# A fused attention and mixture-of-experts layer: expert blocks in four passes instead of two, with 48 instead of 32 tiles of sums beside them, and a shorter plan

## The chip, the cores and the metric

The kernel runs on one core of one Trainium2 chip. The metric is device time in microseconds (us), the median of the runs shown; lower is better. The engines are TensorE (PE, its weight loads PEld), VectorE (DVE), ScalarE (ACT), GpSimd (POOL) and SyncE (SP), which here only issues DMAs.

## The reference

The input x is 16 batches of 512 tokens of 256 values, float32. With `xn = layernorm(x)` the output is

```python
out = x + attention(xn) + moe(xn)
# attention: 16 heads of 16, rope, causal softmax, output projection
# moe, for all 8192 tokens:
scores = softmax(flat @ router_w.T + router_bias)            # 32 experts
topk_scores, topk_idx = top_k(scores, 4); topk_scores /= topk_scores.sum()
h = silu(x @ gate_w[e].T) * (x @ up_w[e].T)                  # hidden width 128
out = sum over the 4 chosen e of topk_score * (h @ down_w[e].T)
out += (silu(flat @ sgate_w.T) * (flat @ sup_w.T)) @ sdown_w.T   # shared expert, width 512
```

## The kernel before

`P` is 128, `E` 32 experts, `TOPK` 4, `TOKENS` 8192, `SEQ` 512, `NT` 4 tiles of 128 tokens in a batch.

**Phase A** (`phase_a`) runs the 16 batches one after the other, in an order of steps written out by hand (`ORDER`, and `LAST_ORDER` for the last batch). Each batch gets layernorm, attention, the shared expert and the router. x plus attention plus the shared expert goes to `sum_dram` in device memory. The router's steps `route`, `rank`, `rankA`, `rankB` and `rankC` find for each token and choice a row of `values`, where every expert has a region of its own; four indirect DMAs of GpSimd per tile (line 537) write the normalized token, its destination row and its weight there. A row's place within a region is the number of tokens that chose this expert before: TensorE counts them (`rank`), and VectorE keeps the totals in `both`: `counts` (all tokens so far, line 850) and `early` (those of the first 4096 tokens, line 848, with the mask `in_half` of line 825). `base = counts + region` is line 824.

**The plan** is the head of `phase_bc` (lines 1314 to 1351 and 1422 to 1469). From the two rows of counts it works out, on one row of 288 columns, where each of the `NBLOCK` = 288 blocks of 128 rows starts in `values` (`place`) and which expert it belongs to (`expert`). There are `VE = 2 * E` = 64 runs, one for each half of the tokens and each expert. `past[v, n]` says whether block n lies past the start of run v; three matmuls with one output row (lines 1347 to 1349) sum it over the runs, with one semaphore after the last. Then 14 small VectorE instructions, each waiting for the one before, turn the sums into `place` and `expert` (lines 1450 to 1469) and raise `ready`. SyncE and TensorE start when `ready` is up.

**Stage C**, the blocks, follows in the same function. Block n: SyncE loads its 128 rows (line 1218, four places at a time, up to 16 blocks ahead: it waits until block n - 16 has been scattered); TensorE transposes them (1358), multiplies by the expert's gate and up weights (1369), ScalarE takes tanh (1274), VectorE gates and weights (1483 to 1489), TensorE transposes (1377) and multiplies by the down weights (1383), ScalarE copies the result (1288) and GpSimd scatters it by rows to `y_dram` (1329), four rows for each token. All experts' weights lie in SBUF, so a change of expert loads nothing. The loop has 16 blocks ahead, 8 iterations of `BODY` = 32 blocks (`LOOPS` = 8), and 16 blocks behind.

The first half's runs are done after at most `HBLOCK` = 160 blocks. So from iteration `H0` = 5 on, beside every fourth block, one of the first `HTILE` = 32 **tiles of sums** is taken (`tile_half`, `out_half`, lines 1227 to 1242; `half_a`, `half_b`, `half_c`, 1493 to 1506): SyncE loads the tile's four expert results (512 KB) and its row of `sum_dram` (128 KB), VectorE adds them in three instructions, SyncE stores 128 KB to `out`. 8 tiles fall in each of the iterations 5, 6 and 7, and 8 beside the last 16 blocks.

```python
H0 = HBLOCK // BODY
PER = BODY // 4
assert (LOOPS - H0) * PER + PER == HTILE
```

In the same loops `sums_part` loads the sums of the other half of the tokens into SBUF (`sums_in`, four tiles in each iteration).

**Stage D** (`phase_d`) follows all of it. For the other 32 tiles SyncE loads `ys` (line 1561, 512 KB each, four buffers), VectorE adds in three instructions (1582, 1584, 1588) and ScalarE's queue stores `res` to `out` (1569).

Of the kernel before, what the change touches and what calls it, by code (L numbers as in the profile page):

```python
# [34 lines left out]
P = 128  # L35
# [24 lines left out]
HTOK = TOKENS // 2  # L60
HTILE = HTOK // P
HBLOCK = HTOK * TOPK // P + E
# [118 lines left out]
def block_kernel(nc, x, wqkvr, wo, wgu_s, wd_s, bias, wgu_e, wd_e, rope_cos, rope_sin, out):  # L181
# [5 lines left out]
    with ctx:  # L187
# [9 lines left out]
        both = sb("both_counts", [P, 2, E])  # L197
        early, counts = both[:, 0, :], both[:, 1, :]
# [7 lines left out]
        phase_a(nc, sb, sem, ident, iota_e, both, we_gu, we_d, ps_g, ps_u, ps_av, x, wqkvr, wgu_e, wd_e, wo, wgu_s, wd_s, bias,  # L206
                rope_cos, rope_sin, values, sum_dram)
        phase_bcd(nc, sb, sem, ident, iota_e, both, we_gu, we_d, ps_g, ps_u, ps_av, values, sum_dram, y_dram, out)


def phase_a(nc, sb_, sem, ident, iota_e, both, we_gu, we_d, ps_g, ps_u, ps_av, x, wqkvr, wgu_e, wd_e, wo, wgu_s, wd_s, bias,
            rope_cos, rope_sin, values, sum_dram):
    stack = ExitStack()
    early, counts = both[:, 0, :], both[:, 1, :]
    with stack:
# [100 lines left out]
        in_half = sb("in_half", [P, 1])  # L316
# [145 lines left out]
        def _(pool):  # L462
# [25 lines left out]
            const(pool.memset(both[:], 0.0))  # L488
# [180 lines left out]
        def _(dve):  # L669
            front = Chain(dve, dve_front, 2 + 3 + 3 * 3 + 6 + 8, passed_dve)  # L670
# [126 lines left out]

            def route(b, step, env):
# [41 lines left out]
            def rank_b(b, step, env):  # L840
# [279 lines left out]
def phase_bcd(nc, sb_, sem, ident, iota_e, both, we_gu, we_d, ps_g, ps_u, ps_av, values, sum_dram, y_dram, out):  # L1120
    outer = ExitStack()
    with outer:

        sums = sb_("sums_in", [P, HTILE, D], F32, outer)
        stored_h = [sem(f"stored_h{i}") for i in range(NSUM)]
        phase_bc(nc, sb_, sem, ident, iota_e, both, we_gu, we_d, ps_g, ps_u, ps_av, values, sum_dram, y_dram, sums, out, stored_h)
        phase_d(nc, sb_, sem, y_dram, sums, out, stored_h)
# [5 lines left out]
def phase_bc(nc, sb_, sem, ident, iota_e, both, we_gu, we_d, ps_g, ps_u, ps_av, values, sum_dram, y_dram, sums, out, stored_h):  # L1133
    stack = ExitStack()
    with stack:
# [5 lines left out]
        VE = 2 * E  # L1141
        nb_i = sb("nb_i", [P, 2, E], I32)
        nb_f = sb("nb_f", [P, 2, E])
        run_r = sb("run_r", [P, 3, VE])
        first_r = sb("first_r", [P, VE + 1])
        nb_c = sb("nb_c", [VE, 4])
        tri = sb("tri", [VE, VE])
# [38 lines left out]
        H0 = HBLOCK // BODY  # L1186
        PER = BODY // 4
        assert NBLOCK == 2 * NR + LOOPS * BODY and HBLOCK == H0 * BODY
        assert (LOOPS - H0) * PER + PER == HTILE

# [13 lines left out]
        def _(sp):  # L1204
# [15 lines left out]
            def sums_part(i):  # L1220

                nt = HTILE // LOOPS
# [21 lines left out]
            def loop_part(i, tiles, second):  # L1244
                for k in range(BODY):
                    stage(i * BODY + NR + k, k % NR, False)
                    if k == NR:
                        sums_part(i)
                    if tiles and k % 4 == 0:
                        tile_half((i - H0) * PER + k // 4, k // 4, second and k < 4 * NYS, second)  # L1250
# [7 lines left out]
            for n in range(NBLOCK - NR, NBLOCK):  # L1258
                stage(n, n % NR, False)
                if n % 2 == 0:  # L1260
                    s = (n - (NBLOCK - NR)) // 2
                    tile_half(HTILE - PER + s, s, False, False)
# [51 lines left out]
        def _(pool):  # L1314
# [317 lines left out]
```

## Time and profile before

| what | before |
|---|---|
| median of 3 runs | 1873.74 us (1872.81 to 1875.88) |
| the profiled execution's own time | 1873.05 us |
| its span, first to last instruction | 1871.2 us |
| phase A, until the last sums are stored | 0 to about 1273 us |
| the plan, first row of counts to `ready` | 1276.4 to 1290.2 us |
| first to last block (first tanh to last scatter) | 1297.7 to 1796.2 us |
| stage D, first load issued to the end | 1805.4 to 1871.2 us |
| mean granted TensorE clock | 0.955 of full speed |

The profile is one execution of the program, recorded by the hardware. Busy time is given for each engine, the idle time before an instruction with what ended it. TensorE's two levels of clock are 1.2 and 2.4 GHz; a granted clock of 0.5 is the lower one. A matmul's end is modelled, so a busy TensorE is not one at its peak.

### The profile page before, as it was taken

The page shows a single profiled execution, that of the slowest core. Times are in us where ns is not written, and L with a number is a line of the kernel's source. Part 1 is how long each engine was busy: PE and PEld are TensorE (multiplying, and loading weights), DVE is VectorE, ACT ScalarE, POOL GpSimd, SP SyncE. Part 2 cuts the span into 40 slices and gives each one's busy share as a digit, 9 for nine tenths or more (in the row PEclk, how much of TensorE's full clock was granted, in tenths as well). Part 3 has the DMA queues.
Part 4 walks back from the last instruction along what each step waited for, and adds up shares of the span by engine and source line. Part 5 has one row for each costly group of instructions (what it writes and reads, how often), then busy time and mean ns, then how long its engine had stood idle before and what let it go on. Part 6 is the DMA issues. An engine that isn't in the chain of part 4 may idle for free. (4 is left out here: it accounts for less than half of the span.)

```text
span 1871.2 us, 43234 instructions
## 1 busy us (share of the span) xinstructions
PE 1697.6 (91%) x11827; PEld 1052.2 (56%) x11828; DVE 1358.2 (73%) x3501; ACT 794.2 (42%) x1667; POOL 710.4 (38%) x716
## 2 busy tenths in 40 slices
PE   4999999999999999999999999686999999999930
PEld 2455554554555545545555455344877888777720
DVE  5977878779778797797887977534666666777857
ACT  2544445344453454444534544231444444444410
POOL 5433423334233243342332433301555565555520
PEclk8999999999999999999999999767999999999975
DMA  7273561743725617437266173684555555788958
GB/s 144 76 127 58 112 113 42 128 70 90 124 54 114 93 58 135 62 98 124 46 119 83 70 130 60 153 229 148 165 166 154 165 174 171 244 259 255 299 185 315
DMA packets 171641, 253.18 MB, mean 135 GB/s; under 512 B 25269, under 2 KB 121406, under 8 KB 171584
## 3 DMA queue, kind: packets, MB, share of 16 engines
q1 hardware_dynamic: 128256, 168.34, 42.5%
q0 software_dynamic: 26112, 67.42, 9.8%
q10 hardware_dynamic: 17216, 16.78, 3.0%
q8 instruction: 21, 0.34, 0.1%
q14 instruction: 36, 0.29, 0.1%
HBM read 112.54 MB, written 92.70 MB: 110 GB/s over the span
## 5 line engine op out<-in xcount | busy, mean ns | idle before, releaser
L752 DVE TENSOR_REDUCE neg<-ps_u 128x2 f32<-128x768 f32 (+3 forms) x384 | 389.7, 1042 | 65.2 <-PE ps_u L1009 60.4
L537 POOL DMA_INDIRECT values<-we_gu,slot x256 | 250.0, 977 | 381.9 <-ACT we_gu L609 227.9
L1329 POOL DMA_INDIRECT y_dram<-yb_all,xg x288 | 283.5, 984 | 235.2 <-issue 162.9
L987 PE MATMUL ps_g<-we_gu 128*128 128x512 f32 x512 | 251.9, 620 | 0.0
L629 ACT ACTIVATE probs<-ps_u 128x1024 f32<-128x1024 f32 x160 | 160.3, 1023 | 166.9 <-PE ps_u L1050 166.9
L1003 PE MATMUL ps_u<-k_st,q_st 48*128 48x128 f32 (+3 forms) x1024 | 177.5, 392 | 39.3 <-ACT we_d L629 26.9
L629 ACT ACTIVATE we_d<-ps_u 128x1024 f32<-128x1024 f32 x160 | 159.4, 1021 | 111.1 <-PE ps_u L1050 100.6
L527 POOL TENSOR_TENSOR we_gu<-we_d,we_gu 128x512 fp32r<-128x512 f32 x64 | 81.9, 1290 | 286.1 <-ACT we_gu L577 286.1
L1003 PEld LDWEIGHTS ps_u<-k_st,q_st 48*128 48x128 f32 x1024 | 88.0, 189 | 156.0 <-DVE neg L752 74.6
L1383 PE MATMUL ps_u<-we_d,h_t 128*128 x576 | 175.2, 386 | 0.0
L1036 PE MATMUL ps_u<-q_st,k_st 50*128 50x512 f32 (+3 forms) x1024 | 158.9, 375 | 8.5 <-DVE neg L752 2.9
L1036 PEld LDWEIGHTS ps_u<-q_st,k_st 50*128 50x128 f32 x1024 | 83.8, 190 | 143.2 <-issue 52.2
L1369 PE MATMUL ps_g<-we_gu,x_t 128*128 x576 | 150.7, 384 | 4.7 <-issue 4.7
L1369 PE MATMUL ps_av<-we_gu,x_t 128*128 x576 | 150.2, 383 | 1.6 <-issue 1.4
L1483 DVE TENSOR_SCALAR wh<-xg 128x1 f32<-128x1 f32 x288 | 44.3, 154 | 142.6 <-ACT tnh L1274 120.6
L601 ACT ACTIVATE we_gu<-ps_g 128x512 f32<-128x512 f32 x64 | 37.8, 591 | 231.6 <-PE ps_g L987 231.6
L987 PEld LDWEIGHTS ps_g<-we_gu 128*128 128x128 f32 x512 | 89.1, 191 | 80.5 <-issue 75.7
L1476 DVE COPY x_t<-ps_g 128x256 f32<-128x256 f32 x288 | 120.5, 418 | 10.1 <-PE ps_g L1358 8.2
L968 PE MATMUL ps_g<-we_gu 128*128 128x512 f32 x256 | 126.5, 617 | 0.0
L1080 PE MATMUL ps_u<-w_d,hid 128*128 128x256 f32 x512 | 125.6, 395 | 0.0
L1288 ACT ACTIVATE yb_all<-ps_u 128x256 f32<-128x256 f32 x288 | 110.6, 384 | 33.8 <-PE ps_u L1383 8.0
L518 POOL TENSOR_TENSOR we_d<-we_d 128x512 f32<-128x512 f32 x64 | 81.8, 1279 | 106.9 <-DVE we_d L722 104.0
(188 smaller groups left out, 2892.3 us busy)
## 6 DMA issues: line engine op xcount, KB each, us to landing
xg<-values SPq DMA_DIRECT2D x288, 129.0 KB
q_st<-we_gu SPq DMA_DIRECT2D x192, 128.0 KB, 4.1
k_st<-we_gu SPq DMA_DIRECT2D x192, 128.0 KB, 6.5
ys_h<-y_dram SPq DMA_DIRECT2D x32, 512.0 KB
ys<-y_dram SPq DMA_DIRECT2D x32, 512.0 KB, 5.4
we_gu<-x SPq DMA_DIRECT2D x16, 512.0 KB
xres<-x SPq DMA_DIRECT2D x16, 512.0 KB, 9.7
sum_dram<-osum SPq DMA_DIRECT2D x16, 512.0 KB, 9.2
```

The source lines that it names most:

```text
L537: pool.indirect_dma_start(values[:, :], bass.IndirectOffsetOnAxis(ap=slot[:, k:k + 1], axis=0), xs[:, t % 2, j, :], None).then_inc(scatter ...
L629: nc.scalar.activation(probs[g % 2][:, u, :], ps_u[env[1][step][0]][:, :, :].rearrange("p a n -> p (a n)"), ACT.Exp, scale=SCALE).then_inc ...
L752: nc.vector.tensor_reduce(neg[:, g % 2, i, :, k0:k0 + nk], ps[:, :, 0:nk * n].rearrange("p a (k n) -> p a k n", n=n), AX.X, ALU.max, negat ...
L968: ins = nc.tensor.matmul(ps[:, :], w_qkvr[:, c, lo:lo + P], xn_t[:, c, :], start=(c == 0), stop=(c == KC - 1))
L987: ins = nc.tensor.matmul(ps[:, :], w_gu[:, c, lo:lo + P], xn_t[:, c, :], start=(c == 0), stop=(c == KC - 1))
L1003: nc.tensor.matmul(ps[:, a, k * n:(k + 1) * n], q_st[rows, h, i * P:(i + 1) * P], k_st[rows, h, 0:n], start=(k == 0), stop=False, skip_gro ...
L1036: nc.tensor.matmul(ps[:, a, lo:lo + n], k_st[rows, h, kt * P:(kt + 1) * P], q_st[rows, h, kt * P:SEQ], start=(lo == 0), stop=False, skip_g ...
L1080: nc.tensor.matmul(ps[:, t // 2, (t % 2) * D:(t % 2 + 1) * D], hid[:, m, t * P:(t + 1) * P], w_d[:, m, :], start=(t % 2 == 0 and m == 0), ...
L1329: pool.indirect_dma_start(y_dram[:, :], bass.IndirectOffsetOnAxis(ap=ent[k][:, 0:1], axis=0), yb[k][:, :], None, bounds_check=TOKENS * TOP ...
L1369: ins = nc.tensor.matmul(ps_gu[s][:, 0:2 * HE], x_t[s][:, c * P:(c + 1) * P], w_gu[:, bass.ds(e, 1), c, :], start=(c == 0), stop=(c == KC ...
L1383: nc.tensor.matmul(ps_y[s][:, 0:D], h_t[s][:], w_d[:, bass.ds(e, 1), :], start=True, stop=True).then_inc(y_ps, 1)
L1476: nc.vector.tensor_copy(x_t[s][:], ps_x[s][:, 0:D]).then_inc(xt_sb, 1)
```

## The change

- Stage C takes the blocks in four equal passes of four batches (`MARKS` = 4, 8, 12, 16 batches) instead of two halves. A pass takes, for each expert, the blocks that its tokens have filled up to the mark. The number of blocks stays 288. 
- The tiles of sums start in iteration `H0` = 3 instead of 5, still one beside every fourth block: `HTILE` is 48 instead of 32, 8 in each of the iterations 3 to 7 and 8 beside the last 16 blocks. Stage D has `LTILE` = 16 tiles instead of 32, and `sums_part` loads two tiles in each iteration instead of four.
- Phase A keeps the counts after each batch in `seen[:, b + 1, :]`, addressed by the loop's register, instead of `early` and `counts`. Lines 825 and 848 go, with one link of VectorE's chain.
- The plan has `VE` = 128 runs. Its arithmetic per run (the step from one run to the next, in blocks and in experts) stands in columns of 128 values (`step_e`, `step_p` by GpSimd; `col_p`, `col_m` by VectorE), and four matmuls, each with a semaphore count of its own, give the sums of these. 7 VectorE instructions on the row of 288 follow instead of 14.

```diff
-HTOK = TOKENS // 2
+MARKS = (4, 8, 12, BATCH)
+NPASS = len(MARKS)
+HTOK = MARKS[-2] * SEQ
 HTILE = HTOK // P
-HBLOCK = HTOK * TOPK // P + E
+LTILE = TOKENS // P - HTILE
...
-        both = sb("both_counts", [P, 2, E])
-        early, counts = both[:, 0, :], both[:, 1, :]
+        seen = sb("seen", [P, BATCH + 1, E])
...
+            def seen_by(b):
+                return seen[:, bass.ds(b, 1), :].rearrange("p o e -> p (o e)")
...
-                front.link(b, nc.vector.tensor_tensor(base[:], counts[:], region[:], ALU.add))
-                front.link(b, nc.vector.tensor_scalar(in_half[:], dest_f[:, 0:1], float(HTOK * TOPK), None, ALU.is_lt))
+                front.link(b, nc.vector.tensor_tensor(base[:], seen_by(b), region[:], ALU.add))
...
-                new = ps_g[bank][:, NT * E:(NT + 1) * E]
-                nc.vector.scalar_tensor_tensor(out=early[:], in0=new, scalar=in_half[:, 0:1], in1=early[:], op0=ALU.mult,
-                                               op1=ALU.add)
-                nc.vector.tensor_tensor(counts[:], counts[:], new, ALU.add
+                nc.vector.tensor_tensor(seen_by(b + 1), seen_by(b), ps_g[bank][:, NT * E:(NT + 1) * E], ALU.add
                                         ).then_inc(S["ranked"], 1)
...
-        VE = 2 * E
+        VE = NPASS * E
...
-        H0 = HBLOCK // BODY
-        PER = BODY // 4
-        assert (LOOPS - H0) * PER + PER == HTILE
+        H0, EVERY = 3, 4
+        PER, LAST = BODY // EVERY, NR // 2
+        assert (LOOPS - H0) * PER + LAST == HTILE
+
+        def block_of(t):
+            return NR + H0 * BODY + EVERY * t if t < HTILE - LAST else NBLOCK - NR + 2 * (t - (HTILE - LAST))
+        for lo, hi in zip((0,) + MARKS, MARKS[:-1]):
+            assert block_of(lo * NT) // 4 * 4 >= hi * NT * TOPK + E + NR
...
-                nt = HTILE // LOOPS
+                nt = LTILE // LOOPS
...
+            pool.memset(step_e[:], 1.0).then_inc(c_pool, 1)
             pool.memset(tri[:], 0.0).then_inc(c_pool, 1)
-            pool.wait_ge(c_pool, 5)
+            pool.wait_ge(c_pool, 6)
 
             pool.affine_select(out=tri[:], in_=tri[:], compare_op=ALU.is_ge, fill=1.0, base=-1,
                                pattern=[[-1, VE]], channel_multiplier=1).then_inc(c_pool, 1)
+            for p in range(1, NPASS):
+                pool.affine_select(out=step_e[:], in_=step_e[:], compare_op=ALU.not_equal, fill=float(1 - E),
+                                   base=1 - E * p, pattern=[[0, 1]], channel_multiplier=1).then_inc(c_pool, 1)
+                pool.wait_ge(c_pool, 7 + p)
+            pool.affine_select(out=step_p[:], in_=step_e[:], compare_op=ALU.not_equal, fill=float(4 * BLANK // RB),
+                               base=1 - VE, pattern=[[0, 1]], channel_multiplier=1).then_inc(c_pool, 1)
+            pool.affine_select(out=step_e[:], in_=step_e[:], compare_op=ALU.not_equal, fill=0.0,
+                               base=1 - VE, pattern=[[0, 1]], channel_multiplier=1).then_inc(c_pool, 1)
...
-            pe.wait_ge(plan, 4)
-            nc.tensor.matmul(ps_g[0][0:1, 0:NBLOCK], one_c[:], past[:], start=True, stop=True)
-            nc.tensor.matmul(ps_av[0:1, 0:NBLOCK], nb_c[:, 2:3], past[:], start=True, stop=True)
+            pe.wait_ge(plan, 5)
             nc.tensor.matmul(ps_g[2][0:1, 0:NBLOCK], nb_c[:, 1:2], past[:], start=True, stop=True).then_inc(plan_pe, 1)
+            nc.tensor.matmul(ps_av[0:1, 0:NBLOCK], col_m[:], past[:], start=True, stop=True).then_inc(plan_pe, 1)
+            nc.tensor.matmul(ps_g[0][0:1, 0:NBLOCK], col_p[:], past[:], start=True, stop=True).then_inc(plan_pe, 1)
+            nc.tensor.matmul(ps_g[1][0:1, 0:NBLOCK], step_e[:], past[:], start=True, stop=True).then_inc(plan_pe, 1)
...
+            dve.wait_ge(c_pool, 7 + NPASS + 1)
+            dve.wait_ge(plan, 2)
+            nc.vector.scalar_tensor_tensor(out=col_p[:], in0=step_p[:], scalar=float(RB), in1=nb_c[:, 1:2], op0=ALU.mult,
+                                           op1=ALU.subtract)
+            nc.vector.tensor_scalar(col_m[:], step_e[:], float(-RB), None, ALU.mult).then_inc(plan, 1)
+            dve.wait_ge(plan, 3)
+            nc.vector.scalar_tensor_tensor(out=col_m[:], in0=nb_c[:, 2:3], scalar=3.0, in1=col_m[:], op0=ALU.mult,
+                                           op1=ALU.add)
...
+            link(nc.vector.scalar_tensor_tensor(out=row_f[:, 0, :], in0=blk_i[0:1, :], scalar=float(-CB),
+                                                in1=ps_g[2][0:1, 0:NBLOCK], op0=ALU.add, op1=ALU.is_ge))
+            dve.wait_ge(plan_pe, 4)
+            link(nc.vector.scalar_tensor_tensor(out=row_f[:, 1, :], in0=ps_av[0:1, 0:NBLOCK], scalar=float(E * RB - CB),
+                                                in1=row_f[:, 0, :], op0=ALU.add, op1=ALU.mult))
+            link(nc.vector.tensor_tensor(row_f[:, 1, :], row_f[:, 1, :], blk_i[0:1, :], ALU.add))
+            dve.wait_ge(plan_pe, 5)
+            link(nc.vector.tensor_tensor(row_f[:, 1, :], row_f[:, 1, :], ps_g[0][0:1, 0:NBLOCK], ALU.add))
             link(nc.vector.tensor_scalar(row_f[:, 1, :], row_f[:, 1, :], float(BLANK), None, ALU.min))
+            nc.vector.tensor_copy(place[:], row_f[:, 1, :])
+            dve.wait_ge(plan_pe, 6)
+            nc.vector.tensor_copy(expert[:], ps_g[1][0:1, 0:NBLOCK]).then_inc(ready, 1)
...
-        NTILE = HTILE
+        NTILE = LTILE
```

## Rows read from the trace of the kernel before

**Rows 1.** The page: busy time by engine; granted clock in 40 slices, in tenths
```profile
PE 1697.6 (91%) x11827; PEld 1052.2 (56%) x11828; DVE 1358.2 (73%) x3501; ACT 794.2 (42%) x1667; POOL 710.4 (38%) x716
...
PEclk8999999999999999999999999767999999999975
```

**Rows 2.** The chain of waits from 1780 us on: shares of the chain by line
```profile
by line: DMA ys<-y_dram 36.2%; DVE red L1582 12.7%; DVE red L1584 8.1%; DVE res L1588 5.0%; issue 4.4%; DVEq L1588 0.9%; SPq L1561 0.5%; DVEq L1583 0.4%; DVEq L1552 0.3%; DVEq L1581 0.3%
```

**Rows 3.** Windows: length, busy (count) of PE, PEld, DVE, ACT, POOL; PEclk, DMA share, GB/s
```profile
1433.57:1488.20 54.63, 53.32 (x290) 44.10 (x290) 33.27 (x128) 26.77 (x97) 31.48 (x33) 1.00 0.53 164
...
1597.28:1652.73 55.45, 54.14 (x289) 44.00 (x289) 43.09 (x152) 26.76 (x96) 31.41 (x33) 1.00 0.81 250
1652.73:1708.08 55.35, 54.03 (x289) 44.01 (x289) 43.14 (x152) 26.89 (x96) 31.59 (x33) 1.00 0.79 252
1708.08:1764.95 56.87, 55.86 (x296) 45.09 (x296) 44.44 (x157) 27.79 (x99) 31.79 (x33) 1.00 0.92 290
...
1793.75:1809.20 15.45, 0.00 (x0) 0.00 (x0) 0.00 (x0) 0.01 (x1) 1.97 (x2) 0.62 0.20 70
1809.22:1837.90 28.68, 0.00 (x0) 0.00 (x0) 23.97 (x48) 0.00 (x0) 0.00 (x0) 0.50 0.97 348
```

**Rows 4.** Timeline, VectorE, stage D: start us, length us, instruction [idle before <-releaser]
```profile
1809.22 0.69 DVE L1582 TENSOR_TENSOR red<-ys 128x512 f32<-128x512 f32 x1 [16.62 <-DMA ys<-y_dram]
...
1834.27 0.68 DVE L1582 TENSOR_TENSOR red<-ys 128x512 f32<-128x512 f32 x1
...
1835.90 0.68 DVE L1582 TENSOR_TENSOR red<-ys 128x512 f32<-128x512 f32 x1
...
1837.93 0.69 DVE L1582 TENSOR_TENSOR red<-ys 128x512 f32<-128x512 f32 x1 [0.32 <-DMA ys<-y_dram]
...
1866.95 0.68 DVE L1582 TENSOR_TENSOR red<-ys 128x512 f32<-128x512 f32 x1
```

**Rows 5.** Timeline of all engines through the plan
```profile
1276.36 0.80 DVE L1429 TENSOR_SCALAR nb_f<-both_counts 128x64 f32<-128x64 f32 x1 [3.48 <-PEq L215]
...
1277.26 0.23 POOL L1323 TENSOR_SCALAR_AFFINE_SELECT tri<-tri 64x64 f32<-64x64 f32 x1
...
1281.01 1.12 PE L1347 MATMUL ps_g<-yb_all,one_c 64*1 64x288 f32 x2 [0.64 <-DVE yb_all L1447]
...
1282.88 1.16 PE L1349 MATMUL ps_g<-yb_all,nb_c 64*1 64x288 f32 x2
...
1284.08 0.44 DVE L1450 TENSOR_TENSOR yb_all<-yb_all,ps_g 1x288 f32<-1x288 f32 x1 [3.13 <-PE ps_g L1349]
...
1288.87 0.30 DVE L1466 TENSOR_SCALAR yb_all<-yb_all 1x288 f32<-1x288 f32 x1
...
1289.87 0.30 DVE L1469 CAST expert<-yb_all 1x288 int32<-1x288 f32 x1
```

**Rows 6.** Timeline of VectorE in one batch of phase A, where counts are taken
```profile
1074.09 0.19 DVE L824 TENSOR_TENSOR base<-both_counts,region 128x32 f32<-128x32 f32 x1
1074.31 0.15 DVE L825 TENSOR_SCALAR in_half<-dest_f 128x1 f32<-128x1 f32 x1
...
1081.92 0.29 DVE L830 TENSOR_REDUCE zs<-exo 128x4 f32<-128x128 f32 x1 [3.19 <-ACT exo L634]
...
1084.76 0.28 DVE L845 TENSOR_TENSOR pos<-ps_g,base 128x128 f32<-128x128 f32 x1
1085.08 0.25 DVE L848 SCALAR_TENSOR_TENSOR both_counts<-ps_g,in_half,both_counts 128x32 f32<-128x32 f32 x1
...
1088.22 0.72 DVE L773 STREAM_TRANSPOSE av<-ps_av 128x512 f32<-128x512 f32 x1 [2.80 <-PE ps_av L1068]
```

**Rows 7.** Line 1588, VectorE's sequencer: count, duration in ns (min/median/max)
```profile
L1588 DVEq FUSED_REGOPS  x28: 57/57/57, 1817.1 to 1868.1; - x28
```

**Rows 8.** Line 1329, GpSimd: 1400 to 1560 us, without tiles
```profile
L1329 POOL DMA_INDIRECT y_dram<-yb_all,xg x94: 982/984/992, 1400.3 to 1559.1; - x94
```

**Rows 9.** The same line from 1600 to 1760 us, with tiles
```profile
L1329 POOL DMA_INDIRECT y_dram<-yb_all,xg x94: 982/984/1107, 1599.4 to 1759.8; - x94
```

More of the change, by code:

```diff
@@ L204, in block_kernel, with phase_a @@
         ps_av = ctx.enter_context(nc.psum_tensor("ps_av", [P, 512], F32))
-        phase_a(nc, sb, sem, ident, iota_e, both, we_gu, we_d, ps_g, ps_u, ps_av, x, wqkvr, wgu_e, wd_e, wo, wgu_s, wd_s, bias,
+        phase_a(nc, sb, sem, ident, iota_e, seen, we_gu, we_d, ps_g, ps_u, ps_av, x, wqkvr, wgu_e, wd_e, wo, wgu_s, wd_s, bias,
                 rope_cos, rope_sin, values, sum_dram)
-        phase_bcd(nc, sb, sem, ident, iota_e, both, we_gu, we_d, ps_g, ps_u, ps_av, values, sum_dram, y_dram, out)
-def phase_a(nc, sb_, sem, ident, iota_e, both, we_gu, we_d, ps_g, ps_u, ps_av, x, wqkvr, wgu_e, wd_e, wo, wgu_s, wd_s, bias,
+        phase_bcd(nc, sb, sem, ident, iota_e, seen, we_gu, we_d, ps_g, ps_u, ps_av, values, sum_dram, y_dram, out)
+def phase_a(nc, sb_, sem, ident, iota_e, seen, we_gu, we_d, ps_g, ps_u, ps_av, x, wqkvr, wgu_e, wd_e, wo, wgu_s, wd_s, bias,
             rope_cos, rope_sin, values, sum_dram):
     stack = ExitStack()
-    early, counts = both[:, 0, :], both[:, 1, :]
+    counts = seen[:, BATCH, :]
     with stack:
@@ L315, in phase_a @@
         dest_f = sb("dest_f", [P, NT * TOPK])
-        in_half = sb("in_half", [P, 1])
         xs = in_gu([P, 2, TOPK, ROW])
@@ L487, in _ @@
                             allow_small_or_imprecise_dtypes=True))
-            const(pool.memset(both[:], 0.0))
+            const(pool.memset(seen[:], 0.0))
             const(pool.memset(over[:], 0.0))
@@ L1146, in phase_bc @@
         nb_c = sb("nb_c", [VE, 4])
+        step_e = sb("step_e", [VE, 1])
+        step_p = sb("step_p", [VE, 1])
+        col_p = sb("col_p", [VE, 1])
+        col_m = sb("col_m", [VE, 1])
         tri = sb("tri", [VE, VE])
@@ L1185, in phase_bc @@
         LOOPS = (NBLOCK - 2 * NR) // BODY
-        H0 = HBLOCK // BODY
-        PER = BODY // 4
-        assert NBLOCK == 2 * NR + LOOPS * BODY and HBLOCK == H0 * BODY
-        assert (LOOPS - H0) * PER + PER == HTILE
+        H0, EVERY = 3, 4
+        PER, LAST = BODY // EVERY, NR // 2
+        assert NBLOCK == 2 * NR + LOOPS * BODY
+        assert (LOOPS - H0) * PER + LAST == HTILE
[3 more added lines that the diff above has]
+            assert block_of(lo * NT) // 4 * 4 >= hi * NT * TOPK + E + NR
         def expert_loop(eng, stage):
@@ L1248, in loop_part @@
                         sums_part(i)
-                    if tiles and k % 4 == 0:
-                        tile_half((i - H0) * PER + k // 4, k // 4, second and k < 4 * NYS, second)
+                    if tiles and k % EVERY == 0:
+                        q = k // EVERY
+                        tile_half((i - H0) * PER + q, q % NSUM, second and q < NYS, second and q < NSUM)
             for n in range(NR):
@@ L1428, in link @@
                 dve.wait_ge(dchain, n_[0])
-            link(nc.vector.tensor_scalar(nb_f[:], both[:], float(P - 1), None, ALU.add))
+            link(nc.vector.tensor_scalar(nb_f[:], seen[:, MARKS[0]:BATCH + 1:MARKS[0], :], float(P - 1), None, ALU.add))
             link(nc.vector.tensor_copy(nb_i[:], nb_f[:]))
@@ L1466, in _ @@
             link(nc.vector.tensor_scalar(row_f[:, 1, :], row_f[:, 1, :], float(BLANK), None, ALU.min))
-            link(nc.vector.tensor_copy(place[:], row_f[:, 1, :]))
-            link(nc.vector.tensor_scalar(row_f[:, 0, :], row_f[:, 3, :], float(E - 1), None, ALU.min))
-            nc.vector.tensor_copy(expert[:], row_f[:, 0, :]).then_inc(ready, 1)
+            nc.vector.tensor_copy(place[:], row_f[:, 1, :])
+            dve.wait_ge(plan_pe, 6)
+            nc.vector.tensor_copy(expert[:], ps_g[1][0:1, 0:NBLOCK]).then_inc(ready, 1)
@@ L1511, in loop_part @@
                     stage(i * BODY + NR + k, k % NR, False)
-                    if tiles and k % 4 < 3:
-                        [half_a, half_b, half_c][k % 4]((i - H0) * PER + k // 4, k // 4)
+                    if tiles:
+                        q = k // EVERY
+                        t, s = (i - H0) * PER + q, q % NSUM
+                        if k % EVERY == 0:
+                            half_a(t, s)
+                        elif k % EVERY == 1:
+                            half_b(t, s)
+                        if k % EVERY == min(2, EVERY - 1):
+                            half_c(t, s)
             front(0, 0, True)
```

50 lines of the change are left out of this document (18 added, 32 removed).

## The prediction

> **What bounds the kernel now.** I read the page first. TensorE is busy 91% of the span, VectorE 73%, and the granted clock is full except in three slices around 1220 to 1320 us and at the very end [rows 1]. An average over the span says little here: the change touches the counts of phase A, the plan, the blocks and stage D, and each has a limit of its own.
>
> The chain that ended last lies wholly in stage D: 36.2% of what it covers is the wait for the loads of `ys`, the rest VectorE's three additions for each tile [rows 2]. TensorE, ScalarE and GpSimd do nothing in that stage; only the DMA engines (0.97 busy, 348 GB/s) and VectorE work [rows 3]. So a tile of stage D costs its full time, and a tile beside the blocks costs only what it adds to them.
>
> The windows of stage C are cut at the tanh of blocks 16, 48, 80 and so on, one window for each iteration of 32 blocks. Iteration 2 (from 1433.57 us) has no tiles and takes 54.63 us; TensorE is busy 53.32 us of it, with VectorE at 33.27 us and the DMA engines at 0.53. The four other iterations without tiles are as long within 0.25 us. Iterations 5, 6 and 7 carry 8 tiles each: 55.45, 55.35 and 56.87 us, VectorE at 43 to 44 us, DMA at 0.79 to 0.92 [rows 3]. TensorE bounds the blocks with and without tiles.
>
> Between the phases the plan is one serial chain, during which TensorE waits: its first row instruction starts at 1284.08 us, when the third matmul is done, and the last starts at 1289.87 us [rows 5].
>
> **The change, part by part.** The sum is made against the profiled execution's own time, 1873.05 us, 1.85 us above its span; the median shown is 0.69 us above it.
>
> *Stage D: 16 tiles fewer.* The first addition starts at 1809.22 us, the 16th tile's at 1835.90, the 32nd's at 1866.95 [rows 4]. What stands before the first (a gap of 15.45 us from the last result copied to the first addition, nearly empty [rows 3]) and after the last stays. If stage D is cut after its 16th tile, 1866.95 - 1835.90 = 31.05 us go. Bounds: the fastest a tile can be is where the data is there, from 1834.27 to 1835.90, 1.63 us, VectorE's own pace; 15 such steps are 24.5 us, and of the 57.73 us now 33.2 would go. The slowest 15 steps are those of the second half, 1837.93 to 1866.95, 29.02 us: 28.7 us would go. I take 31.05, because the new stage starts from idle queues just as the old one's first half does.
>
> *Stage C: 16 tiles more.* Iterations 3 and 4 become what 5 and 6 are now: the same 8 tiles, 24 additions and 8 times 768 KB. That is 55.40 - 54.63 = 0.77 us each, 1.5 us in all. The upper end is iteration 7, 56.87 - 54.63 = 2.24 us each, 4.5 in all; but its second half holds also the loads for the last 16 blocks, which take a tile for every second block, and SyncE runs up to 16 blocks ahead. The lower end is 0: `sums_part` moves half as much. SyncE's queue gains in each iteration 8 stores, which wait for VectorE's addition, and the rows for later blocks are queued behind them; in iterations 5 and 6 the same waits cost no more than the 0.77 us, since the blocks' rows are loaded up to 16 ahead. The order of the blocks changes, with four runs of each expert instead of two; no weights are loaded for a run, so I cost it at nothing.
>
> *The plan.* Before, the first of the three matmuls started at 1281.01 us and they followed each other at half of 1282.88 - 1281.01, 0.94 us; the first took 1.12 us [rows 5]. Let t be the start of the first. Before, `ready` rose at 1289.87 + 0.30, t + 9.16. Now each matmul signals for itself, ready at t + 1.1, 2.1, 3.0 and 4.0. The first row instruction starts at t + 1.15; a linked one costs 0.48 us, as from 1284.08 over the ten steps to 1288.87 [rows 5]. The second starts with the second matmul at t + 2.1, the third follows at 2.6, the fourth at 3.1 (the third matmul is done), the minimum at 3.55, the copy of `place` at 3.9, and the copy of `expert`, after the fourth matmul, at about 4.1, done by 4.6. So t + 4.6 instead of t + 9.2: 4.6 us less. Against it: eight instructions ahead of t work on 64 columns more. A column costs (0.28 - 0.19) / 96, 0.9 ns, by lines 845 and 824 [rows 6], so 8 times 64 columns are 0.5 us. The two or three small instructions for `col_p` and `col_m` (0.15 us each, as line 825) stand where VectorE waits for the matmul with `tri`; some 0.1 us may stick out. GpSimd's five added selects run beside VectorE: at 0.23 us as line 1323 and some 0.15 us for each wait they end near 1279.2 us, 0.7 us before VectorE needs them. That makes -4.0 us. Bounds: -5.0 (the wider rows cost nothing), and -2.5, if GpSimd is 1.5 us slower than that.
>
> *Phase A.* Lines 825 and 848 go. Their room on VectorE is 0.20 us (1074.31 to the next at 1074.51) and 0.16 us (1085.08 to 1085.24) in each batch. But VectorE idles right behind both places, 3.19 us for ScalarE's exponentials before line 830 and 2.80 us for TensorE before line 773 [rows 6], so nothing comes of it. If all of it did, 16 times 0.36 = 5.8 us would go. Three operands now take their address from a register; the nearest row is the register arithmetic of line 1588, 57 ns [rows 7], so at most 16 times 3 times 0.057 = 2.7 us would come, hidden by the same idle time. I take 0.
>
> *Sum:* -31.05 + 1.5 - 4.0 + 0 = -33.5 us, 1873.05 - 33.5 = 1839.5 us. With half of the 0.69 us to the median I give 1840.
>
> *One rule against the change.* GpSimd's scatter instruction takes 984 ns at the median without tiles [rows 8] and 984 ns with them, at most 1107 [rows 9], although VectorE is busy about 9.8 us more in an iteration there (43.09 against 33.27 [rows 3]), all of it additions with two SBUF inputs. The Trainium skill says otherwise for such a pair (SBUF — State Buffer, "Who interferes with whom"): a VectorE instruction with two SBUF inputs contends with a GpSimd instruction that reads SBUF, and the second to start is blocked until the first is done. By that rule each of the new additions could stand behind a scatter. It is the last rival below, priced from rows.
>
> **Rivals.**
>
> *A. The extra tiles cost more.* All five iterations with tiles become like iteration 7, because the DMA engines (0.92 there) are the ones that stretch a block. Then 3 and 4 cost 4.5 us, and 5 and 6 another 1.5 each: 6.0 us above my term, 1845.5 us. For it speaks that iteration 7 exists; against it that 5 and 6, with the same tiles, stay at 0.8 [rows 3].
>
> *B. TensorE's clock moves.* Over the last batch of phase A and the plan the granted clock is 0.6 to 0.7 on average, that is partly at 1.2 and partly at 2.4 GHz [rows 1]. A slightly different timing of VectorE may shift these stretches by some us of TensorE work either way: 1833 or 1847 us, by 7 us, about a sixth of one slice of 46.8 us. The runs shown are 3 us apart already.
>
> *C. Slower.* The lock on a shared port decides. VectorE's additions for tiles and GpSimd's scatters collide in iterations 3 and 4: 16 tiles, 48 additions, each held up by a scatter of 0.98 us [rows 8] and passed on to TensorE in full. That is 47 us, and 1839.5 - 1.5 + 47 gives 1885 us. It decides from 33.5 + 1.5 = 35 us on, 0.73 us for each addition. Against it: 24 additions cost an iteration 0.77 us in all today, 0.03 us each [rows 3], and the scatters are as long with them as without [rows 9].
>
> *D. No change.* Stage D would have to be bound by something that is not its tiles, such as the stores waiting for their end. Its chain shows loads and additions alone [rows 2], so this is barely possible: 1873 us.
>
> **How the numbers follow.** My forecast 0.79, A 0.09, B 0.09, C 0.02, D 0.01. The terms' bounds, taken together as if independent, give about 6 us below and 5 above 1839.5; with B's 7 us the range is 1833 to 1847, which takes in A. A measurement of this kernel tells 0.2% (3.7 us) from no change. Faster by more than that: 0.79 + 0.09 + 0.09 = 0.97; the same 0.01; slower 0.02.
>
> **What the new profile would show.** Stage D with 16 instructions of line 1582's kind, some 27 us from the first to the last; iterations 3 to 6 at about 55.4 us each; `ready` about 4 us earlier, counted from the plan's first instruction, with the row instructions starting 3 us before the last matmul's end; phase A ending within some us of 1273. I am wrong if an iteration with tiles takes over 57 us, if the plan's first row instruction is held up by GpSimd, if a tile in stage D takes 2 us or more, or if the batches of phase A change by more than 0.3 us each.

## The result and the profile after

| | before | after |
|---|---|---|
| median, with the kernel before run beside it | 1874.81 us (4 runs) | 1857.05 us (4 runs, 1853.3 to 1861.08) |
| the profiled execution's own time | 1873.05 us | 1861.08 us |
| its span | 1871.2 us | 1859.2 us |

The ratio is 0.9903, with a 95% interval of 0.988 to 0.9925. The change makes the kernel 17.8 us faster, where 33.5 were forecast; 1857 lies outside the range of 1833 to 1847. The profiled execution of the changed kernel is the longest of its four, 4.0 us above the median, so the stages below add up to 12.0 us and not to 17.8.

The page, its span, busy times and granted clock (before in [rows 1]):

```profile
span 1859.2 us, 43225 instructions
...
PE 1704.5 (92%) x11829; PEld 1054.9 (57%) x11830; DVE 1349.1 (73%) x3465; ACT 793.5 (43%) x1667; POOL 711.8 (38%) x722
...
PEclk8999999999999999999999999876899999999995
```

Windows of the changed kernel's stage C, one for each iteration (2, 3, 4, 5 and 6), columns as in [rows 3]:

```profile
1396.68:1451.09 54.41, 53.29 (x290) 44.21 (x290) 33.24 (x128) 26.79 (x97) 31.31 (x33) 1.00 0.53 160
1505.36:1560.48 55.12, 54.00 (x290) 44.10 (x289) 43.11 (x152) 26.78 (x96) 31.81 (x33) 1.00 0.83 257
1560.48:1616.18 55.70, 54.40 (x290) 44.07 (x289) 43.13 (x152) 26.99 (x96) 31.47 (x33) 1.00 0.82 254
1616.18:1671.62 55.44, 53.70 (x289) 43.88 (x288) 43.05 (x152) 26.66 (x96) 31.59 (x33) 1.00 0.85 272
1671.62:1727.24 55.62, 54.30 (x290) 44.15 (x290) 43.02 (x152) 26.93 (x96) 31.44 (x33) 1.00 0.84 259
```

Iteration 2 has no tiles. Iterations 3 and 4 now carry them, at 55.12 and 55.70 us; before, 5 and 6 took 55.45 and 55.35 [rows 3]. All eight iterations together took 438.8 us before and take 440.0 now.

Stage D, VectorE's timeline: the first and the last of the 16 tiles.

```profile
1827.78 0.69 DVE L1607 TENSOR_TENSOR red<-ys 128x512 f32<-128x512 f32 x1 [16.21 <-DMA ys<-y_dram]
...
1854.91 0.69 DVE L1607 TENSOR_TENSOR red<-ys 128x512 f32<-128x512 f32 x1
```

27.1 us from the first to the last, where [rows 4] has 57.73 for 32: 30.6 us less.

The plan, timeline of all engines:

```profile
1298.09 0.42 DVE L1448 TENSOR_SCALAR nb_f<-seen 128x128 f32<-128x128 f32 x1 [6.23 <-PEq L216]
...
1300.84 0.19 POOL L1341 TENSOR_SCALAR_AFFINE_SELECT step_e<-step_e 128x1 f32<-128x1 f32 x1
...
1302.87 0.37 DVE L1474 TENSOR_SCALAR yb_all<-yb_all,nb_c 128x288 f32<-128x288 f32 x1
...
1303.29 1.12 PE L1365 MATMUL ps_g<-yb_all,nb_c 128*1 128x288 f32 x2 [0.65 <-DVE yb_all L1474]
...
1304.45 0.44 DVE L1476 SCALAR_TENSOR_TENSOR yb_all<-yb_all,ps_g 1x288 f32<-1x288 f32 x1 [1.21 <-PE ps_g L1365]
...
1305.48 0.45 DVE L1479 SCALAR_TENSOR_TENSOR yb_all<-ps_av,yb_all 1x288 f32<-1x288 f32 x1 [0.59 <-PE ps_av L1366]
...
1307.47 0.44 DVE L1487 CAST expert<-ps_g 1x288 int32<-1x288 f32 x1
```

From the start of the first matmul with one output row (1303.29) to the end of `expert` (1307.91) it is 4.62 us; it was 9.16 [rows 5]. VectorE's first row instruction starts right after the first of the four matmuls and not after the last. GpSimd's last select starts at 1300.84, ahead of the columns' first use. From the plan's first instruction to that matmul it is 5.20 us; it was 4.65. The whole plan took 13.81 us and takes 9.82.

So far nothing is missing. It is missing in phase A. Its last instruction, before and after:

```profile
1272.18 0.69 DVE L794 TENSOR_TENSOR osum<-ps_u,xres 128x512 f32<-128x512 f32 x1 [1.03 <-PE ps_u L1089]
```

```profile
1291.17 0.69 DVE L794 TENSOR_TENSOR osum<-ps_u,xres 128x512 f32<-128x512 f32 x1 [1.03 <-PE ps_u L1088]
```

Phase A ends 19.0 us later. The first instruction of the plan then waits 6.23 us for the end of the phase instead of 3.48 [rows 5]; the trace names no more than TensorE's sequencer for it. The changed kernel's last step from `base` to `base`, that is from one batch to the next (line 827 there, 824 before):

```profile
1090.01 0.19 DVE L827 TENSOR_TENSOR base<-seen,region 128x32 f32<-128x32 f32 x1
...
1104.14 0.72 DVE L773 STREAM_TRANSPOSE av<-ps_av 128x512 f32<-128x512 f32 x1 [2.84 <-PE ps_av L1067]
...
1125.28 1.41 DVE L683 BATCH_NORM_STATS2 stats<-we_gu 128x6 f32<-128x256 f32 x4 [0.70 <-DMA we_gu<-x]
...
1166.73 0.18 DVE L827 TENSOR_TENSOR base<-seen,region 128x32 f32<-128x32 f32 x1
```

And the same part of an earlier batch of the kernel before, the next `base` of which is at 1074.09 [rows 6]:

```profile
998.94 0.18 DVE L824 TENSOR_TENSOR base<-both_counts,region 128x32 f32<-128x32 f32 x1
...
1033.40 1.40 DVE L683 BATCH_NORM_STATS2 stats<-we_gu 128x6 f32<-128x256 f32 x4
```

The two steps are 76.72 and 75.15 us long, but they are not the same one: the last step before took 76.53. Over all 15 steps the median goes from 75.17 to 76.33 us and the sum from 1120.1 to 1135.5. So 15.3 of the 19.0 us come in the loop; 0.8 come ahead of its first `base` and 2.9 in the last batch, behind its last. The counts' own instructions are shorter, as expected, and the idle time behind them longer: line 773 waits 2.84 us where it waited 2.80 [rows 6]. The loss is elsewhere: line 683, the first instruction of the layernorm of the next batch, now waits for the load of x. All waits for DMAs between 100 and 1160 us, before and then after (engine, line, what it waited for: us in total, times, longest):

```profile
ACT we_gu L609 <- DMA values<-we_gu,slot: 32.7, 16, 3.4
...
DVE stats L683 <- DMA we_gu<-x: 0.2, 1, 0.2
```

```profile
ACT we_gu L609 <- DMA values<-we_gu,slot: 48.5, 15, 4.2
...
DVE stats L683 <- DMA we_gu<-x: 12.2, 14, 2.0
```

And the copies between SBUF tensors that fill `q_st` and `k_st` (line 415), which stand ahead of the sums, `xres` and x on SyncE's queue. Time from issue to landing, before and then after:

```profile
DMA to landing us min/median/max: 2.9/5.3/7.7
```

```profile
DMA to landing us min/median/max: 3.2/5.6/8.1
```

Nothing in the change touches these copies, except where they lie. `seen` takes 2176 bytes of each partition where `both` took 256, so every tensor of phase A allocated later begins 1920 bytes further on in SBUF.

### The profile page after: what moved, and what is told of

It is laid out like the page before. It is cut to its first block and busy times, and to the rows that moved or that the text cites. A ratio compares the mean times of both kernels' runs of the same rounds, so it can differ in the third digit from the quotient of the medians.

```text
span 1859.2 us, 43225 instructions
## 1 busy us (share of the span) xinstructions
PE 1704.5 (92%) x11829; PEld 1054.9 (57%) x11830; DVE 1349.1 (73%) x3465; ACT 793.5 (43%) x1667; POOL 711.8 (38%) x722
## 3 DMA queue, kind: packets, MB, share of 16 engines
q1 hardware_dynamic: 130816, 170.44, 44.4%
```

## The experiments

Three theories. **L** (layout): the addresses make the copies slower, and what is queued behind them comes late. **V**: the counts' new instructions, addressed from a register and in another place of VectorE's order, cost the time. **C**: the profile of the changed kernel is from a slower moment or chip.

The runs fall in groups with a time of the kernel before beside each. In two groups it took 1875 to 1876 us, as in the first measurement; in three it took 1970 to 1980 us. The runs carry the number of their chip: 0 and 3 for the first two, 14, 8 and 8 for the other three. So the level goes with the chip as far as it was seen, but no chip was seen at both levels and only one was used twice; that the chip causes it is not shown. I compare within a group alone.

### Where the kernel before takes 1970 to 1980 us

**The kernel before, unedited** (e0_control).

> The kernel before, unedited, for a profile of it from the same chip as the runs beside it. Theory L (the 1920 bytes that the counts grew by move every later SBUF tensor, and the SBUF-to-SBUF copies into q_st and k_st run slower from the new addresses): batches of phase A last 75.15 us as in the first profile, and the load of x is waited for almost nowhere. Theory C (the profile of the changed kernel comes from a slower chip or moment): batches last about 76.3 us here too, and VectorE's line 683 waits for the load of x. Time by L 1873 to 1878 us with the copies at 5.3 us median to landing; by C the same time on a slower chip, with 5.6 us.

Measured: 1981.05 us beside 1980.26. Its batches last 82.3 us at the median. The longest waits that no other engine or DMA in the profile ends, and the one for the scatters:

```profile
ACT neg_t L620 <- remote: 75.4, 11, 8.0
...
DVE neg L752 <- remote: 49.6, 15, 4.4
...
ACT we_gu L609 <- DMA values<-we_gu,slot: 4.6, 3, 3.4
```

In one batch VectorE stands still for 4.28 us ahead of line 752, and ScalarE for 3.10 us beside it:

```profile
998.50 0.19 DVE L824 TENSOR_TENSOR base<-both_counts,region 128x32 f32<-128x32 f32 x1
...
1039.40 0.96 DVE L752 TENSOR_REDUCE neg<-ps_u 128x2 f32<-128x768 f32 x1 [4.28 <-remote]
```

The view names the releaser "remote", which says no more than that. I read it so that these stalls cover much of what comes late behind the copies: line 683 waits for x only once, in the first batch. No run tests this reading.

**The kernel before with shifted tensors** (e1_before_shift1920 and, in the next group, f1_before_shift1920).

```diff
         both = sb("both_counts", [P, 2, E])
+        shift = sb("shift", [P, 480])
```

> The kernel before with 1920 unused bytes behind the counts, so that every later SBUF tensor of phase A lies where the changed kernel has it, and nothing else. Theory L: the batches grow from 75.15 to about 76.3 us and the whole by 14 to 18 us, ratio to before 1.008 to 1.010. Theory C and theory V (the cost comes from the counts' new instructions, their addresses from a register or their new place in VectorE's order): no change, ratio 0.998 to 1.002.

> The kernel before with 1920 unused bytes behind the counts, again. Where the kernel before takes some 1874 us, theory L expects batches of 76.3 us and 1888 to 1892 us, ratio 1.007 to 1.010, with the copies' 2048-byte packets at a mean of 260 ns instead of 253; theory V (the counts' instructions) 1874 us, ratio 1.000. Where it takes some 1980 us both expect 1.000, as measured.

Measured: 1.0006 (0.9983 to 1.0029) and 1.0002 (0.9979 to 1.0026). No cost here. By time alone theory L would have fallen; it stood because of the packets' duration, below.

**The changed kernel with 128 bytes more** (e2_after_shift128, f2_after_shift128), which puts each later tensor of phase A 2048 bytes beyond its old place:

```diff
         seen = sb("seen", [P, BATCH + 1, E])
+        shift = sb("shift", [P, 32])
```

> The changed kernel with 128 unused bytes behind the counts, so that the later tensors of phase A lie exactly 2048 bytes beyond their place in the kernel before, at the same offset from each multiple of 512. Theory L, if alignment is what matters: batches of 75.1 us again, the whole at about 1840 us, ratio 0.981 to 0.984. Theory V or C: as the changed kernel, ratio about 0.990.

> The changed kernel with 128 unused bytes behind the counts, again. Where the kernel before takes some 1874 us, theory L expects batches of 75.1 us, 1838 to 1842 us, ratio 0.981 to 0.983, packets at 253 ns; theory V 1857 us, 0.990. Where it takes some 1980 us both expect 0.984.

**The changed kernel itself** (f0_after).

> The changed kernel itself beside the others of this group. Where the kernel before takes some 1874 us: about 1857, ratio 0.990, batches of 76.3 us. Where it takes some 1980 us, as in the first group: theory L expects the misplaced SBUF tensors to cost nothing there, because other waits cover them, so -31 for stage D, -4 for the plan and +1.5 for stage C: ratio 0.983 to 0.985.

Measured: 0.9841 (0.9793 to 0.989) and 0.9852 (0.9823 to 0.9881) with the 128 bytes, 0.9856 (0.9829 to 0.9884) without. At this level the changed kernel gains 27 us as it is and 28 to 30 us with the 128 bytes; the intervals overlap, so the 128 bytes give nothing that can be told. The late x isn't covered altogether: in f0 line 683 still waits for it 6 times between 100 and 1160 us, 4.6 us in all, against 12.2 us in 14 batches at the other level.

**Two passes** (e3_two_passes, and h3_two_passes_shift128 with the 128 bytes as well): the counts and the plan of the change, without its tiles.

```diff
-MARKS = (4, 8, 12, BATCH)
+MARKS = (8, BATCH)
...
-        H0, EVERY = 3, 4
+        H0, EVERY = 5, 4
```

> The changed kernel with two passes instead of four (marks at batches 8 and 16, tiles of sums from iteration 5 on, 32 of them): what is left of the change are the counts of phase A in one tensor of 17 rows and the shorter plan. The addresses of phase A are those of the changed kernel. Theory L and theory V both expect batches of 76.3 us, so +17 us, and the plan -4 us: ratio 1.006 to 1.008. Theory C: -4 us, ratio 0.997 to 0.999.

> Two passes instead of four, with the 128 unused bytes: phase A's new counts and the shorter plan, at addresses like those of the kernel before. Theory L and the working of the prediction: only the plan's 4 us go, batches of 75.15 us, ratio 0.997 to 0.999 where the kernel before takes some 1874 us. If the counts' instructions cost or save more than 2 us over the batches, the ratio leaves that.

Measured: 0.9962 (0.9938 to 0.9986) and 0.9967 (0.9948 to 0.9986), 7 to 8 us less than before. The plan's 4 us lie inside both intervals. For e3 theories L and V both had 1.006 to 1.008, and both missed; only C's 0.997 to 0.999 comes near. But at this level a shift that costs 13.6 us at the other (g1, below) can't be measured either, so neither of these two runs can speak against V.

**All copies at multiples of 512 bytes** (f4_after_all512): the 128 bytes, and

```diff
-        bias_bc = sb("bias_bc", [P, E])
...
-        row_p = sb("row_p", [P, 1])
...
-        w_qkvr = in_gu([P, KC, 3 * D + E])
...
         parts = in_gu([P, NPART, NCH, SEQ])
+        w_qkvr = in_gu([P, KC, 3 * D + E])
...
         v_pad = sb("v_pad", [P, NT, NH, 2 * DH])
+        bias_bc = sb("bias_bc", [P, E])
+        row_p = sb("row_p", [P, 1])
```

> The changed kernel with 128 unused bytes behind the counts, the bias and one small column moved behind v_pad and the weights w_qkvr behind parts, so that parts, q_st and k_st all start at a multiple of 512 bytes. If the copies' speed goes by the offset within 512 bytes, their packets fall below 253 ns and the time is that of the kernel with 128 bytes or up to 5 us less; if only some offsets are bad and the kernel before has none of them, the two are the same within 2 us.

Measured: 0.9867 (0.9843 to 0.9892), the same as the others in time; its packets are in the table below.

**One side at a time** (h1_q512: the moves of `bias_bc` and `row_p` without that of `w_qkvr`; h2_parts512: that of `w_qkvr` alone), one execution each.

> The changed kernel with 128 unused bytes behind the counts and the bias and one column moved behind v_pad, so that the copies' destinations q_st and k_st start at a multiple of 512 bytes and their source parts stays 256 bytes beyond one. Packets of 2048 bytes took 253 ns with (source, destination) at (256, 160) beyond a multiple of 512, 260 at (128, 32), 246 at (0, 0). If the destination alone sets the speed: 246 ns here. If the source alone: 253. If both add: 249 to 250.

> The same with the source alone at a multiple of 512 (w_qkvr behind parts) and the destinations 160 bytes beyond one. Source alone sets it: 246 ns. Destination alone: 253. Both add: 249 to 250.

Measured: 1935.44 and 1936.55 us, a single run of each, which the spread of several us in this group makes useless as a time. Their packets count.

### Where the kernel before takes 1875 us

**The kernel before with shifted tensors** (g1_before_shift1920), the edit of e1.

> The kernel before with 1920 unused bytes behind the counts. Where the kernel before takes some 1874 us: theory L 1888 to 1892 us, ratio 1.007 to 1.010, batches of 76.3 us, line 683 waiting for x; theory V 1.000. Where it takes some 1980 us: 1.000, as twice measured.

Measured: 1889.64 us beside 1876.09, ratio 1.0073 (1.0056 to 1.009): 13.6 us slower by 1920 unused bytes. Its waits for DMAs, and its longest step from batch to batch (76.73 us; the median of the 15 is 76.37; line numbers are one higher):

```profile
ACT we_gu L610 <- DMA values<-we_gu,slot: 45.7, 16, 3.7
...
DVE stats L684 <- DMA we_gu<-x: 9.7, 13, 0.8
```

```profile
933.80 0.18 DVE L825 TENSOR_TENSOR base<-both_counts,region 128x32 f32<-128x32 f32 x1
...
1010.53 0.18 DVE L825 TENSOR_TENSOR base<-both_counts,region 128x32 f32<-128x32 f32 x1
```

The signature is that of the changed kernel: x is waited for 13 times, the scatters 45.7 us. Theory V has nothing to say here, for this kernel has none of the counts' new instructions. C falls too, since the kernel before runs beside it at its usual time.

**The changed kernel with 128 bytes more** (g2_after_shift128), the edit of e2.

> The changed kernel with 128 unused bytes behind the counts. Where the kernel before takes some 1874 us: theory L 1838 to 1842 us, ratio 0.981 to 0.983; theory V 0.990. Where it takes some 1980 us: 0.985, as twice measured.

Measured: 1842.38 us, ratio 0.9824 (0.9808 to 0.9841). All of the change is still there, 128 bytes are added, and 15 us are back (1857.05 less 1842.38, each with its own runs of the kernel before beside it). Waits for DMAs, and one step from batch to batch (75.15 us; the median is 75.17, as in the kernel before):

```profile
ACT we_gu L610 <- DMA values<-we_gu,slot: 33.6, 16, 3.4
```

```profile
1000.37 0.19 DVE L828 TENSOR_TENSOR base<-seen,region 128x32 f32<-128x32 f32 x1
...
1075.52 0.18 DVE L828 TENSOR_TENSOR base<-seen,region 128x32 f32<-128x32 f32 x1
```

No wait for x is left between 100 and 1160 us. The two times are of different groups, but the next run, in this same group and with the changed kernel's addresses, has a ratio of 0.9895.

**x ahead of xres** (g3_after_x_first): the changed kernel with SyncE's two loads exchanged.

```diff
+                    if env[0].get((("xT", 0), 0)):
+                        x_load(b + 1)
                     sp.wait_ge(S["sums"], 2 * b)
                     sp.dma_start(xres[:, :, :], tokens(x, b)).then_inc(x_res, 16)
-                    if env[0].get((("xT", 0), 0)):
-                        x_load(b + 1)
```

> The changed kernel with SyncE's two loads of a batch exchanged: the next batch's x is queued ahead of xres, so it lands some 1 to 3 us earlier behind the slower copies. Theory L (copies slower by address, then x late, then VectorE's statistics late): where the kernel before takes some 1874 us, the batches return to about 75.2 us and the whole to 1840, ratio 0.981 to 0.983. Theory V (the counts' instructions themselves): as the changed kernel, 0.990. Where the kernel before takes some 1980 us: as the changed kernel there, 0.986, since line 683 waits for x nowhere.

Measured: 1856.44 us, ratio 0.9895 (0.9878 to 0.9912): nothing gained, so theory L as I had put it was wrong in its last link. The waits show the second path:

```profile
ACT we_gu L609 <- DMA values<-we_gu,slot: 47.7, 16, 3.7
...
DVE gth L731 <- ACT we_gu L601: 15.1, 14, 1.5
```

Line 683 no longer waits for x. But ScalarE's line 609, which fills the rows to be scattered, waits for GpSimd's scatters as long as in the changed kernel (47.7 us; 48.5 there, 32.7 in the kernel before), then line 601 comes late, and VectorE waits for it at line 731: 15.1 us in 14 batches, where it was 2.5 us in 5. The changed kernel's page gives the packets of both as shares of the same 16 DMA engines: 44.4% of their span for the queue with the copies, 10.0% for the scatters'. I read it so that two waits stand beside each other behind one backlog, and taking one out brings up the other.

**Both mends** (g5_all512_x_first), f4's moves and g3's.

> Both mends together: the changed kernel with parts, q_st and k_st at multiples of 512 bytes and x loaded ahead of xres. Where the kernel before takes some 1874 us, 1835 to 1840 us, ratio 0.979 to 0.982, by theory L; 0.989 by theory V. Where it takes some 1980 us, 0.984 to 0.987 by both.

Measured: 1841.59 us, ratio 0.9815 (0.9798 to 0.9831), the same as with the 128 bytes alone. The wait for the scatters falls further, to 28.2 us, and nothing comes of it: once the copies are as fast as before the change, faster ones give phase A nothing that can be measured.

**Which side of the copies** (i1_src128_dst160, i2_src256_dst32). i1 has the 128 bytes behind `we_d` in place of `seen`; i2 has them behind `seen`, and `bias_bc` behind `v_pad`.

> The changed kernel with 128 unused bytes behind we_d: the source parts stays where the changed kernel has it, 128 bytes beyond a multiple of 512, and the destinations q_st and k_st go back to 160 bytes beyond one, as in the kernel before. If the source's place causes the slower copies, packets stay at 260 ns, and where the kernel before takes some 1874 us the time stays near 1857, ratio 0.990. If the destination's place does, 253 ns and 1842 us, 0.982.

> The reverse: source parts back at 256 bytes beyond a multiple of 512, destinations at 32 bytes beyond one as in the changed kernel. If the source's place causes the slower copies, 253 ns and (before at 1874) 1842 us; if the destination's does, 260 ns and 1857 us.

Measured: 1845.25 us, 0.9839 (0.9821 to 0.9856), and 1852.82 us, 0.988 (0.9862 to 0.9898). Waits for DMAs of i1 and then of i2:

```profile
ACT we_gu L610 <- DMA values<-we_gu,slot: 37.4, 16, 3.5
```

```profile
ACT we_gu L610 <- DMA values<-we_gu,slot: 44.0, 16, 3.6
...
DVE stats L684 <- DMA we_gu<-x: 8.8, 14, 0.9
```

With the destination put back, the wait for x is gone; with the source put back, it stays. The edits move other tensors too: i1 puts back all that is allocated behind `we_d`, and i2 leaves off its old place what lies between `bias_bc` and `v_pad`. Of the tensors that DMAs write in every batch, `xres` is at its old offset in i2, and x, which lies in `we_gu`, is at its new one in i1; `q_st` and `k_st` alone go with the wait. i1 was to take 1842 us by theory L and i2 1857: the one is 3 us above, the other 4 below.

Over all kernels, the mean duration of the 25,088 packets of 2048 bytes in each trace (24,576 of them are the copies'), by where source and destination start beyond a multiple of 512 bytes:

```
kernels                                    source  destination   mean ns
f4, g5                                          0            0   246.7, 246.3
h1                                            256            0   246.8
h2                                              0          160   254.1
before, e0, e2, f2, g2, h3                    256          160   253.2 to 253.8
i1                                            128          160   253.5
i2                                            256           32   259.9
after, e1, f0, g1, e3                         128           32   258.8 to 260.5
```

The destination alone sorts them, at either level of the kernel's time. Three offsets of it were tried: 0, 32 and 160. By how much the kernels' offsets differ follows from their edits; the offsets themselves rest on where the first tensor starts, which no trace shows.

The 8,192 packets of the scatters (4128 bytes each), whose source lies in `we_gu`, are sorted by the other side. Where `we_gu` is at its old offset (before, e0, e2, f2, f4, g2, g5, h1, h2, h3, i2) they last 178.8 to 180.5 ns on average; where it is 128 bytes off (after, e1, e3, f0, f1, g1, g3, i1) 182.0 to 184.6 ns. So the 1920 bytes slow two streams, the copies by their destination and the scatters by their source. i1 mends the first alone, i2 the second alone: that is the way in which their times leave the forecasts, but no run shows that the scatters' few ns are the cause.

## Why the prediction was wrong

- *Stage D* was right: 30.6 us went, 31.05 were forecast. The shares of the chain were read slightly wrong, without effect on the sum: 36.2% is the share of the whole window from 1780 us, while the chain begins at 1805.38; of the chain itself the loads are about half and the additions over a third.
- *Stage C* was right: 1.2 us more over the eight iterations, 1.5 forecast. Rivals A and C do not occur: iterations 3 and 4 stay at 55.1 and 55.7 us, and GpSimd's scatter takes 982 ns at the median there as without tiles. Rival A and the upper end of 4.5 us rest on a misread row: the window taken for iteration 7, 56.87 us, ends at 1764.95, but the tanh of block 272, where it should end, is earlier:

```profile
1763.16 0.28 ACT L1274 ACTIVATE tnh<-ps_g 128x128 f32<-128x128 f32 x1 [0.86 <-PE ps_g L1369]
```

So iteration 7 took 55.08 us, less than 5 and 6; it takes 55.07 now.
- *The plan* was right in each step: 4.62 us from the first matmul where I had 4.6, 0.55 us more ahead of it where I had 0.6, 3.99 less in all where I had 4.0. The bound of -5.0 does not follow from its reason: with wider rows at no cost the sum gives -4.6.
- *Rival D* did not occur either. *Rival B*, the clock, occurs on a smaller scale than its 7 us. The last batch of phase A, from its `base` to the last instruction, in the kernel before, the changed one and the changed one with 128 bytes more (g2), columns as in [rows 3]:

```profile
1150.61:1272.87 122.26, 99.95 (x694) 56.28 (x688) 55.66 (x113) 37.10 (x43) 20.61 (x20) 0.78 0.79 190
```

```profile
1166.73:1291.86 125.13, 100.99 (x692) 56.69 (x688) 55.36 (x111) 37.09 (x43) 20.58 (x20) 0.77 0.78 180
```

```profile
1152.02:1271.62 119.60, 94.49 (x694) 53.06 (x688) 55.35 (x110) 36.87 (x43) 20.58 (x20) 0.83 0.80 191
```

The changed kernel's last batch takes 2.9 us more at nearly the same granted clock (0.77 and 0.78), g2's takes 2.7 us less at a higher one (0.83), with TensorE busy 94.5 us instead of 100.0; these are single executions. What moves these stretches the runs don't show. The three slices with a lower clock lie at 1170 to 1310 us, not around 1220 to 1320.
- *Phase A* is the step that failed. I took 0, bounded by 5.8 us less and 2.7 more, and it was 19.0 more in the profiled execution, 15.3 of them in the loop, with 2.7 more until the plan begins. It is one of the signs of being wrong that the prediction names: batches changed by more than 0.3 us, namely by 1.2 at the median. I had costed the instructions of the change there, and these do cost nothing: the changed kernel with 128 bytes more has batches of 75.17 us at the median and 1120.7 us for the 15 steps, where the kernel before has 75.17 and 1120.1. Its time, 1842.38 beside 1876.09, is 33.7 us less, where 33.5 were forecast; that it is so close is in part luck, for the interval is 30 to 36 us, and its profile holds 2.7 us less in the last batch and a wait 1.9 us longer ahead of the plan. What I had not costed is the declaration `seen = sb("seen", [P, BATCH + 1, E])`: 1920 bytes ahead of almost every other tensor. I had read phase A's queues for the work that the change adds to them and not for the slack that they have. The kernel before has its x just in time: 0.2 us of waiting in 14 batches, with 2.6% more on each copy's packets enough to turn it into 12.2 in the changed kernel, and into 8.8 in i2, where the copies alone are slower.

The Trainium skill has a rule that touches this (DMA: Bandwidth & Descriptors, "How a descriptor splits into AXI transactions"): a descriptor that doesn't start at a multiple of 256 bytes fetches the bytes from the boundary below it as well, so it costs more. For the copies' source the runs show nothing of it: 128 bytes beyond a multiple of 256 gives 253.5 ns (i1), on one it is 253.2 to 254.1 ns with the same destination. For the scatters' source they show a small cost, 2 to 5 ns of some 180. For the copies' destination they show a cost, and one that does not grow with the offset: 32 bytes cost twice what 160 do.

What stays open: why 32 bytes beyond a boundary are worse than 160; whether the scatters' packets are why i1 is at 1845 and g2, with copies as fast, at 1842 (their intervals overlap); what sets the wait ahead of the plan's first instruction, which is 3.5 us in the kernel before, g5 and i1 and 5.4 to 6.5 us in the changed kernel, g1, g2, g3 and i2, so that neither the copies nor the plan's new code sort it; and what the stalls are that end by "remote" where the kernel before takes 1980 us.

## What to carry to other kernels

A tensor that grows moves all tensors behind it. Before such a change is costed at its instructions, look which DMA write stream arrives just in time, and compare the start of its destination before and after; a pad of 128 bytes gave back 15 us here. Compare the same batch, and then the median over all of them: single batches of the kernel before differ by 1.4 us (its short first one aside), more than the 1.2 us looked for. When a wait is taken out and nothing is gained, list the other waits behind the same queue before the theory is dropped.

## What the runs showed of the hardware

Copies between SBUF tensors in rows of 2048 bytes took 246 ns a packet with destinations at a multiple of 512 bytes, 253 to 254 ns at 160 bytes beyond one and 259 to 260 ns at 32 beyond, whatever their source's place among 0, 128 and 256. The scatters' packets of 4128 bytes took 179 to 180 ns with their source's tensor at its old offset and 182 to 185 ns with it 128 bytes off. And the same kernel took 1875 us in some groups of runs and 1970 to 1980 us in others, with its batches at 75.17 and 82.3 us at the median. At the second level the 13.6 us by which shifted tensors slow the kernel at the first are not to be measured at all.

The version to keep is the changed kernel with 128 bytes more behind `seen`: 1842.38 us, ratio 0.9824 (0.9808 to 0.9841), faster than both kernels.
